# Kept store ring between two stages, fewer clearings, a bracket of 64 and a looped slow path

## The reference, cut to what matters

```python
x = x + jnp.tanh(g_xattn[0]) * _L0_xattn_ref(_layernorm(x), ctx_1024, ctx_1024, ...)
x = x + jnp.tanh(g_ffn[0]) * _L0_ffn_ref(_layernorm(x), controller, f1, f2, bias)
x = x + jnp.tanh(g_xattn[1]) * _L1_xattn_ref(_layernorm(x), ctx_1024, ctx_1024, mask)
x = x + jnp.tanh(g_ffn[1]) * _L1_ffn_ref(_layernorm(x), ln_g, ln_b, w1, w2)

# _L0_ffn_ref: 256 groups of 16 tokens; for each of 64 slots one token of the group is chosen
sel = einsum('btd,btes->besd', grouped, perm)
inner = relu(einsum('besd,desf->besf', sel, f1) + bias)
inter = einsum('besf,esfd->besd', inner, f2)
out = einsum('besd,btes->btd', inter, perm)

# _L1_ffn_ref: both inputs of a product are rounded to 8 bits by a quantile of their magnitudes
amax = maximum(quantile(abs(x), 1 - 0.005), 1e-5)
q = clip(round(x * 127 / amax), -128, 127) * amax / 127
h = gelu(qlinear(layernorm(x), w1)); out = qlinear(h, w2)
```

## Time and profile before

| | us |
|---|---|
| median of three runs | 1350.73 |
| profiled execution | 1349.87 |
| its span | 1347.8 |
| PE busy | 1182.2 (88%) |
| DVE busy | 911.4 (68%) |
| ACT busy | 664.5 (49%) |
| POOL busy | 524.5 (39%) |
| mean granted clock of PE | 0.935 of full |

### The profile page before, as it was taken

How to read it: one execution, slowest core, us unless ns; L and a number is a source line. 1 busy time by engine, 2 the same in 40 slices (tenths; PEclk the granted TensorE clock), 3 DMA queues, 4 the chain that set the end, 5 groups by cost and what they waited for, 6 DMA issues and landing times. The chain is left out here.

```text
span 1347.8 us, 25076 instructions
## 1 busy us (share of the span) xinstructions
PE 1182.2 (88%) x9030; PEld 872.9 (65%) x9030; DVE 911.4 (68%) x2166; ACT 664.5 (49%) x1120; POOL 524.5 (39%) x448
## 2 busy tenths in 40 slices
PE   5899999999999997599999966999992399935998
PEld 5788888888888885476666523566551288932443
DVE  5667767766777775344554332999994699976874
ACT  3344334444443443224434342666774299657992
POOL 1233333333333333248768731476663000002352
PEclk9999999999999998699999987999996599966999
DMA  6222322332222216295887889999923589734994
GB/s 231 80 72 98 115 96 97 107 113 104 94 94 94 94 64 217 98 360 186 301 312 282 293 325 336 370 339 329 325 110 83 109 231 408 317 131 190 418 365 149
DMA packets 127601, 274.25 MB, mean 203 GB/s; under 512 B 44145, under 2 KB 55313, under 8 KB 120849
## 3 DMA queue, kind: packets, MB, share of 16 engines
q1 hardware_dynamic: 113840, 235.14, 49.1%
q0 software_dynamic: 10688, 36.71, 7.7%
q10 hardware_dynamic: 2976, 1.14, 0.3%
HBM read 155.26 MB, written 109.31 MB: 196 GB/s over the span
## 5 line engine op out<-in xcount | busy, mean ns | idle before, releaser
L1958 PE MATMUL p_z<-qT,w1T 128*128 128x256 bf16 (+1 forms) x1152 | 114.2, 262 | 14.4 <-DMA qT<-p_q 14.3
L1958 PEld LDWEIGHTS p_z<-qT,w1T 128*128 128x128 bf16 x1152 | 102.5, 99 | 25.8 <-DMA qT<-p_q 14.4
L2423 POOL DMA_DIRECT2D p_y<-residual x32 | 26.7, 835 | 230.1 <-POOLq L113 198.6
L379 PE MATMUL p_M<-p_ctxTh,early 128*128 128x256 f32 x512 | 101.0, 291 | 1.9 <-DVE early L712 1.9
L1136 DVE COPY p_selT<-p_sel 128x512 f32<-128x512 f32 x64 | 44.3, 692 | 83.5 <-PE p_sel L989 83.5
L379 PE MATMUL p_M<-p_xnTh,early 128*128 128x256 f32 x512 | 99.0, 287 | 0.6 <-DVE p_V L785 0.6
L2444 PE MATMUL p_o<-w2T,p_Gq 128*128 128x512 bf16 x384 | 86.6, 387 | 6.0 <-DVE p_Gq L2491 6.0
L379 PEld LDWEIGHTS p_M<-p_ctxTh,early 128*128 128x128 f32 x512 | 82.8, 193 | 2.3 <-issue 2.3
L379 PEld LDWEIGHTS p_M<-p_xnTh,early 128*128 128x128 f32 x512 | 80.7, 188 | 3.6 <-issue 3.6
L636 POOL TENSOR_TENSOR p_rs<-p_ve,p_mhalf 128x2 f32<-128x2 f32 x32 | 22.3, 698 | 153.2 <-DVE p_ve L702 153.1
L379 PE MATMUL p_M<-early,p_ctxTh 128*128 128x512 f32 x256 | 81.5, 399 | 0.0
(11 more groups left out here) (373 smaller groups left out, 3266.1 us busy)
## 6 DMA issues: line engine op xcount, KB each, us to landing
inter_d<-p_stage SPq DMA_DIRECT2D x64, 512.0 KB, 4.5
p_rows<-inter_d SPq DMA_DIRECT2D x32, 1024.0 KB, 9.4
activations<-hid SPq DMA_DIRECT2D x20, 1024.0 KB, 7.0
p_cin<-in_ctx_dram SPq DMA_DIRECT2D x32, 512.0 KB, 5.3
xparts<-p_parts SPq DMA_DIRECT2D x16, 768.0 KB, 3.3
activations<-third SPq DMA_DIRECT2D x12, 1024.0 KB, 6.6
hid<-activations SPq DMA_DIRECT2D x12, 1024.0 KB, 14.4
p_xin<-in_x_dram SPq DMA_DIRECT2D x16, 512.0 KB, 4.2
```

The costliest lines, as they stand in the source:

```text
L379: mm = pe.matmul(out, left[a][:, c, lcols], right[e][:, c, rcols], start=(k == 0), stop=(k == len(terms) - 1))
L1958: mm = pe.matmul(bank, w1T[:, c, fc * P:(fc + 1) * P], qT[:, bass.ds(first, tiles), c, :], start=(c == 0), stop=(c == C - 1))
```

## The change

Five edits, in the order of the program.

1. The ring of four slots becomes a tensor (`ring`) that lives through the whole program, and its four semaphores live through gather and joint stage. SP no longer waits for the last stores at the end of the gather stage. In the last block the eight layers of h=0 come first and then those of h=1. In the joint stage `load_rows(0, 0)` waits for 14 stores of each slot (56, all of h=0) and `load_rows(8, 0)` for all 64. The ring also takes the place of several buffers of other stages (inputs of phase 1, junk tiles of the joint stage and of the second search, `q` of product_tops, `y` of ffn).
2. The four semaphores are cleared behind the joint stage (`carried.close()`): a barrier, a clearing and a barrier more than before at that seam.
3. The four stages from `quantile1` on keep their semaphores: their seams are one barrier. One clearing and one barrier stand at the end of the program.
4. SPREAD is 64 instead of 256.
5. DVE's slow path in the first search runs over the 16 pairs in a loop.

```diff
 def semaphores(nc, prefix, names, kept=None):
     sems = {n: nc.alloc_semaphore(prefix + n) for n in names}
     yield sems
     nc.all_engine_barrier()
+    if kept is not None:
+        kept.extend(sems.values())
+        return
     nc.clear_and_free_semaphores(list(sems.values()))
     nc.all_engine_barrier()
+@contextmanager
+def kept_semaphores(nc):
+    kept = []
+    yield kept
+    nc.clear_and_free_semaphores(kept)
+    nc.all_engine_barrier()
-SPREAD = 256
+SPREAD = 64
...
+        def pair_half(n):
+            sb, i = divmod(n, 2 * PAIRS)
+            return (sb, i % PAIRS, i // PAIRS) if sb == NSB - 1 else (sb, i // 2, i % 2)
...
-            for i in range(RING):
-                sp.wait_ge(s[f"stage_out{i}"], 16 * (LAYERS // RING))
...
-                if i % PAIRS == 0:
-                    pe.wait_ge(s[f"f2_in{i // PAIRS}"], 16 * (sb + 1))
+                if h == 0 and j % (PAIRS // 2) == 0:
+                    pe.wait_ge(s[f"f2_in{2 * j // PAIRS}"], 16 * (sb + 1))
...
             def load_rows(b, t):
+                if t == 0 and b in (0, B // 2):
+                    stores = NSB * PAIRS * 2 - (PAIRS if b == 0 else 0)
+                    for done in stage_out:
+                        sp.wait_ge(done, 16 * (stores // len(stage_out)))
...
                 def count_all(i, trial, op):
-                    for k in range(pairs):
-                        magnitudes(k)
-                        dve.tensor_scalar(junk[:, :], junk[:, :], trial, 0.0, op, ALU.add, accum_out=parts[:, k:k + 1]).then_inc(own, 1)
-                        dve.wait_ge(own, m.next(own))
+                    m.apart()
+                    with dve.Fori(0, pairs) as k:
+                        at = i * (2 * pairs) + k * 2
+                        magnitudes(k, at)
+                        dve.tensor_scalar(junk[:, :], junk[:, :], trial, 0.0, op, ALU.add, accum_out=parts[:, bass.ds(k, 1)]).then_inc(passed, 1)
+                        dve.wait_ge(passed, at + 2)
...
+        ring = sbt("ring", [P, 4, NT, D])
+        stage = [ring[:, i, :, :] for i in range(4)]
+        carried = ExitStack()
+        stage_out = list(carried.enter_context(semaphores(nc, "p23_", [f"stage_out{i}" for i in range(4)])).values())
...
+        carried.close()
+        kept = es.enter_context(kept_semaphores(nc))
```

More of the change, by code:

```diff
@@ L106, in semaphores @@
 @contextmanager
-def semaphores(nc, prefix, names):
+def semaphores(nc, prefix, names, kept=None):
     sems = {n: nc.alloc_semaphore(prefix + n) for n in names}
@@ L210, in phase1 @@
         ]
-        xin = [sbt(f"xin{i}", [P, NT, D]) for i in range(2)]
-        cin = [sbt(f"cin{i}", [P, NT, D]) for i in range(2)]
+        xin, cin = [[ring[:, k + i, :, :] for i in range(2)] for k in (0, 2)]
         xb = [sbt(f"xb{i}", [P, NT, D]) for i in range(2)]
@@ L1930, in count_all @@
                     dve.tensor_reduce(slow.cnt[:, :], parts[:, :], AX.X, ALU.add).then_inc(slow.s["asked"], 1)
                 def least_of_all(found):
-                    for k in range(pairs):
-                        magnitudes(k)
-                        dve.tensor_scalar(junk2[:, :], junk[:, :], found, 3e38, ALU.is_le, ALU.mult).then_inc(own, 1)
-                        dve.wait_ge(own, m.next(own))
-                        dve.tensor_tensor(junk[:, :], junk[:, :], junk2[:, :], ALU.max).then_inc(own, 1)
-                        dve.wait_ge(own, m.next(own))
-                        dve.tensor_reduce(parts[:, k:k + 1], junk[:, :], AX.X, ALU.min).then_inc(own, 1)
-                        dve.wait_ge(own, m.next(own))
+                    m.apart()
@@ L1973, with product_tops @@
 GRID_GROUP = BASE_TILE + 2
[L1976 removed]
+def product_tops(nc, hid, qT, w1T, gam, amax, zs, Gs, g_d, cand, K, base, grid, kept, ring):
     rank_here = quantile_ranks(N2)[0] / (NB * P)
@@ L1987, in product_tops @@
         bz = [es.enter_context(nc.psum_tensor(f"p7_z{i}", [P, FC * P], F32)) for i in range(2)]
-        q = [es.enter_context(nc.sbuf_tensor(f"p7_q{i}", [P, 2, D], BF16)) for i in range(QB)]
+        q = [ring[:, i, 0, :].bitcast(BF16).rearrange("p (t d) -> p t d", t=2) for i in range(QB)]
         sbt = lambda n, sh, d=F32: es.enter_context(nc.sbuf_tensor("p7_" + n, sh, d))
@@ L2163, in quantile2 @@
         sbt = lambda n, sh, d=F32: es.enter_context(nc.sbuf_tensor("q2_" + n, sh, d))
-        s = es.enter_context(semaphores(nc, "qb_", "consts at_ready signed counted told own found gelu_done".split()))
-        junk, junk_a = sbt("junk", [P, NC2 - NA], BF16), sbt("junk_a", [P, NA], BF16)
+        s = es.enter_context(semaphores(nc, "qb_", "consts at_ready signed counted told own found gelu_done".split(), kept))
+        flat = lambda a: a.rearrange("p r t d -> p (r t d)").bitcast(BF16)
+        junk, junk_a = flat(ring[:, 0:1, :, :])[:, 0:NC2 - NA], flat(ring[:, 1:3, :, :])[:, 0:NA]
         g, below, signs, cnt, keep, cur, lowest = [sbt(n, [P, 1]) for n in "g below signs cnt keep cur lowest".split()]
@@ L2343, in __getitem__, with ffn @@
         return self.w[p, c, bass.ds(self.first, P)]
-def ffn(nc, Gs, spare, perm, g_d, w2T, gam, amax, gf, x3_d, out_d, cut, small, flag, rows, qT, w1T, zs, K):
+def ffn(nc, Gs, spare, perm, g_d, w2T, gam, amax, gf, x3_d, out_d, cut, small, flag, rows, qT, w1T, zs, K, kept, ring):
     rank, prefix = quantile_ranks(N2)[0], "p8_"
@@ L2357, in ffn @@
         Gq = [sbt(f"Gq{i}", [P, FC, P], BF16) for i in range(QR - 1)] + [perm[:, :, :].rearrange("p t e -> p (t e)").rearrange("p (f n) -> p f n", f=FC)]
-        y = [sbt(f"y{i}", [P, D]) for i in range(YR)]
+        y = [ring[:, i // 2, i % 2, :] for i in range(YR)]
         junk = spare[:, :].bitcast(BF16).rearrange("p (f n) -> p f n", f=FC)
```

81 lines of the change are left out of this document (43 added, 38 removed).

## The result

| | before | after |
|---|---|---|
| median of the runs, us | 1350.55 (1349.06 to 1351.67, 4 runs) | 1333.37 (1331.91 to 1337.03, 4 runs) |
| profiled execution, us | 1349.87 | 1331.91 |
| its span, us | 1347.8 | 1329.9 |

The ratio is 0.9879, 95% interval 0.9863 to 0.9896: faster by 16 us (14 to 18.5), 1.2% of the time and clear of the scatter. The medians differ by 17.2 us and the profiled spans by 17.9; the forecast was 16.4.

What follows compares the result with a forecast made beforehand. The prediction took exposed seams between stages and the second search's chain of rounds as what counts: -4.2+0.8-4.65-1.0+0.3-7.65=-16.4 us, taken off the median of 1350.73 for 1334.3 us, range 1330.5 to 1341.

Steps and rivals of the forecast that it cites:

- The form of the sum: Whole kernel: edits at seams and in the second search are exposed and move everything behind forward; -16.4 us.
- Gather to joint stage: Seam of gather and joint stage: without SP's wait for stores, rows and the whole joint stage start earlier; -4.2 us.
- f2's second half costs nothing at layer 52: Last gather block: f2's second half, needed earlier, lands before layer 52's ring slot is free; cost 0.
- a transfer late by two microseconds: Last gather block: if f2's second half lands two microseconds late, layer 52 costs at most 1 us.
- the order of the halves: Last gather block: first rows wait for only 56 stores, expected done before SP comes there.
- one sign of being wrong: Joint stage: the prediction is wrong if its span counted from SP's start is longer than 227.00 us.
- Seam behind the first search: First search to products: a shorter skipped body removes two instruction-fetch stalls, and a clearing goes; -4.65 us.
- Rival B's half: Seam behind the first search: one of two fetch stalls at DVE's jump stays, 1336.3 us; B whole or half 0.19.
- Clearings: Seams before the first search +0.8 us, before the second -0.6, behind it -0.4, and program end +0.3.
- Second search: Second search: a bracket of 64 takes six halvings instead of eight, all exposed; -7.65 us.
- The range's lower end: Total time: 1330.5 us, below the forecast by 4 for a sooner clock rise, shorter seams and the -5.2 bound.
- Rival D: Second search: the bracket of 64 misses and the whole product is searched; +3500 us or more, about 4850 us; chance 0.03.

Runs made afterwards that it cites:

- 40 more: The new kernel with 40 more instructions, never run, in DVE's looped slow path of the first search, a jump over some 120: 1334.34 us.

## Why the prediction was right

**The form of the sum** (seams and a round chain, all exposed, what is saved there moves the rest) held: all seven terms lie within 0.35 us of what was measured. Putting back SPREAD, the stores' wait and the three clearings gave 7.66, 4.0 and 1.58 us, against the 7.65, 4.2 and 1.6 of the sum. Putting back the unrolled body gave 2.2 of the 4.05 that the sum had beside the clearing.

**Gather to joint stage**, -4.2: -4.14. That the joint stage moves as a whole was right; the first scatter matmul was forecast near 812 and came at 810.45, 1.5 us of which is the scatter ahead. That the difference is only 0.06 is luck: over all traces the wait is worth 3.8 us on SP, with 0.5 us of scatter on either side.

That f2's second half costs nothing at layer 52 held in this trace, with the margin forecast: PE waited 0.62 us for it, and its layer was ready some 0.9 us before the ring slot. The forecast's other case, a transfer late by two microseconds, came in several of the other programs, and in three of them the copy did wait for PE. Wrong was what I took the order of the halves to be for: without it nothing is lost.

By its letter one sign of being wrong came true: the joint stage counted from SP's start is 227.60 us long and not at most 227.00. The sign forgot the forecast's own +0.8 at the seam behind; to ACT's last end the stage has 225.37 us for 225.31.

**Seam behind the first search**, -4.65: -4.34. The reading of the cause was right in kind and the sum came out for a partly wrong reason. Of the 4.34 (by rounding 4.35) are 0.58 a clearing, 2.22 the wait for the target's block, which the loop removes, and 1.55 a wait that goes with a shift by a few instructions. The prediction gave both waits to the body's length, and it counted into the seam a third packet that comes behind it. Rival B's half (2.2 left in the seam) would have come true with a body some 40 to 70 instructions longer; the seam's own part was 2.17 for 1.85, that is 0.3 more for the reading of the flag and the branch.

**Clearings**, +0.8, -0.6, -0.4, +0.3: +0.74, -0.56, -0.42, +0.39.

**Second search**, -7.65: -7.66.

**Total.** The terms make -16.0, and the medians differ by 17.2, the ratio says 14 to 18.5. The rest belongs to no edit: it is within what the stages ahead of the first seam scatter by (4.3 us over the profiled executions). The range's lower end was chosen for a clock that rises sooner; in the stretches that shrink it did not (0.50 in the second search, as before). Over the whole span it was 0.942 for 0.935: less time is left at 0.50, and the stretch at 0.50 from 774.2 to 777.4 is not there in the trace after.

**Rival D** was rightly named and much too cheap: 3500 was a bound of PE's busy time, and the chain of three engines costs five times as much.

## What to carry to other kernels

Where stages are separated by barriers, read the seams first: each wait, clearing and fetch there was in the span in full, and most could be priced to a tenth of a microsecond from one profile, while the totals scatter by several. A seam that is far longer than its neighbours and has a jump over a body that is not run may hold a fetch of instructions; look for packets of the instruction queue in it. Here it helped to shorten what is skipped, and a shift by a few instructions was worth 1.55 us against 2.2 for the whole body. Move a wait for stores behind the barrier to where the data is read before reordering work for it.

## What the runs showed of the hardware

- A jump of DVE over some 120 instructions cost nothing, over 155 and more 2.2 us, without a slope on either side; packets of its instruction queue have 8 KB, and two in a row come 2.4 us apart in the seam of the earlier trace rows. Eight more instructions in the body that is skipped took another 1.55 us away.
- One clearing of semaphores with its barrier took 0.43 us (8 semaphores), 0.57 (26) and 0.58 (those of the first search); twice as many semaphores at the end took 0.39 us more.
- Programs that do the same up to the last store of the gather stage reached it between 798.96 and 803.23 us. The last transfer of f2 (1 MB) took 6.3 to 9.3 us to land in them; where it took at most 6.7, the stage ended by 801.16, and where it took 8.3 or more, at 801.33 or later.
- In four runs (unrolled body, stores' wait, clearings, 40 more) PE stood for 2.65 to 3.37 us ahead of layer 52, and soon behind that its granted clock was 0.50 for some 3.4 us or more; in the run with 40 more the next four matmuls took 2.08 us instead of 1.13.
